# Batch 1's context gate from token pairs, with the weight sums and the steps of x taken by GpSimd in the opening

## The chip, the core and the metric

The kernel runs on one core of one Trainium2 chip. Its engines are TensorE (PE, matrix products), ScalarE (ACT), VectorE (DVE), GpSimd (POOL) and SyncE (SP, which here only issues DMAs). The metric is device time in microseconds (us). The kernel before took 1031.0 us, the median of three runs (1030.94 to 1032.0).

## The reference

Eight batches of 512 tokens with 256 channels pass two layers, each added to its input. What matters for the change is the first layer's context gate:

```python
ctx = causal_ema(x, tau_ctx)              # h[t] = alpha * h[t-1] + x[t]
wg = sigmoid(concat([x, ctx]) @ Wg.T + bg)
gated = x * wg
# then: mod = 0.5 + sigmoid(W2 gelu(W1 x)); eight EMAs of gated * mod, blended, a second gate,
# a projection and a layer norm; x2 = x + that
```

The second layer runs five feed-forward networks per batch (three shared, two experts chosen by the batch's type), each 256 to 1024 to 256 with a relu, and mixes them by a small gate.

## The kernel before, in words

Channels lie on partitions, in two tiles of 128 (CT = 2); tokens lie along the free dimension. Products are exact to nearly fp32: every operand is split into a high part and a low part (`hi` on ACT, `lo` on DVE), and `product` adds three products (high x high, high x low, low x high).

**The mixture sets the pace.** A batch of the second layer is 40 slots. In slot k PE runs `up(k + 2)` (six products into one of four banks `ps_up`), then `down(k)` (six products). Between them ACT computes the relu as the high part `hid_hi` and DVE the low part `hid_lo`; there are four buffers of each. In batch 0 the weights too are split on the way (`wi_round`, `wo_round` on ACT, `wi_rest`, `wo_rest` on DVE) and stored for the later batches.

**The first layer of the next batch runs beside it.** While batch b of the mixture runs, the first layer of batch n = b + 1 is cut into named steps. A plan for each engine says in front of which slot a step stands (k), or behind it (k + 0.5). `FIRST_PLANS` (L82 to L106) is the plan of n = 1, which runs beside batch 0; `PLAN_...` are those of the later ones. Each engine takes its instructions in this order, whatever is ready. A step's `ema_in` and `ema_out` on DVE are the eight EMAs, from slot 3.5 to 23.5 in batch 0.

**The context gate.** Since the EMA is linear, the gate's product can be taken before the scan. For n = 1 (`wgate`, L862) PE takes x and x one token back: for each of two output tiles, four terms of three products of 512 columns (`gate_product`, L810). DVE scans the result out of PSUM (`gate_scan`). For n > 1 the tokens are held apart as evens and odds (256 columns each), and there are two steps: `gate_mid` (L842) multiplies the even tokens by the sum of the two weight matrices, 12 products of 256 columns; `wgate` (L852) multiplies the steps of x (differences of neighbouring tokens) by each weight matrix, 24 products of 256 columns. ACT copies the first result out, DVE adds it to the second and scans (L1524).

**Their inputs.** The summed weights (`mid_raw`) come from `add_gate_weights` on GpSimd (L1929): three additions of 128x512, late in batch 0, between its DMAs for the experts' weights; ACT and DVE split them in slot 38. The steps come from `next_steps` on DVE (L1507): for each channel tile one instruction of one element and two of 255 and 256. ACT and DVE split these too (`next_steps_hi`, `next_steps_lo`).

**The opening.** Before batch 0's mixture can start, the first layer of batch 0 runs alone (to about 54 us). DVE's sixteen scans (L1780) set its pace; the inputs of EMAs 1 to 4 come from PSUM, those of EMAs 0 and 5 to 7 from SBUF (5 to 7 multiplied by GpSimd, L1945). The last one is scanned in halves, with `open_total_end` (L1789) between. Then come a gate, a projection, a layer norm and the split of x2 (`x2_round` on ACT). In the opening x of batch 1 is split as well (`x1_hi`, `x1_lo`), and its soma and hidden layer are computed.

**Between batches**, DVE's `add_expert_b` (L1401) adds the last expert out of `ps_down`; PE's first `down` of the next batch waits for it.

## Time and profile before

| what | value |
|---|---|
| median of three runs | 1031.0 us |
| the profiled execution's own time | 1030.5 us |
| its span (first to last instruction) | 1028.6 us |
| PE busy | 1019.8 us (99%), 4840 products |
| DVE busy | 838.7 us (82%), 1495 instructions |
| ACT busy | 425.7 us (41%) |
| POOL busy | 21.1 us (2%), 29 instructions |
| clock granted to PE | 0.998 of full speed |

The page gives busy time for each engine; a busy PE is not a PE at its peak, since the ends of its products are modelled. Where an engine waited, the list of waits says for whom. The timeline gives single instructions in order of time.

### The profile page before, as it was taken

What the parts mean: (1) busy time and instruction counts of PE and PEld (TensorE: products, weight loads), DVE (VectorE), ACT (ScalarE), POOL (GpSimd) and SP (SyncE); (2) the same over time, 40 slices, a digit from 0 to 9 for tenths busy, and PEclk for the clock granted to TensorE, in tenths of its full rate; (3) what the DMA queues carried; (4) which work ended last, traced back from release to release, by engine and by line L of the source; (5) the groups of instructions that cost most, each with busy time, mean ns of one, the idle gap of its engine ahead of it and who ended that gap; (6) DMA issues with size and microseconds to landing.
All of it is one profiled execution on the core that took longest, in us unless ns stands there. A gap on an engine that the chain in (4) does not pass through costs nothing.

```text
span 1028.6 us, 13022 instructions
## 1 busy us (share of the span) xinstructions
PE 1019.8 (99%) x4840; PEld 850.4 (83%) x4840; DVE 838.7 (82%) x1495; ACT 425.7 (41%) x707; POOL 21.1 (2%) x29
## 2 busy tenths in 40 slices
PE   8999999999999999999999999999999999999998
PEld 6688887888888888888888888888888888888898
DVE  6989978799788988789886997869977799755237
ACT  8654456533444233542435234442334423332232
POOL 1200011000000000000000000000000000000000
PEclk9999999999999999999999999999999999999999
DMA  6387899687354664456544674546645466455682
GB/s 216 104 302 289 304 367 354 251 322 264 135 197 169 242 242 162 165 200 229 192 182 148 236 254 156 205 164 225 231 158 204 165 242 220 141 196 190 220 323 86
DMA packets 38305, 222.53 MB, mean 216 GB/s; under 512 B 4642, under 2 KB 5410, under 8 KB 16610
## 3 DMA queue, kind: packets, MB, share of 16 engines
q1 hardware_dynamic: 35938, 209.12, 56.9%
q0 software_dynamic: 2304, 12.58, 3.1%
q8 instruction: 38, 0.62, 0.2%
q14 instruction: 25, 0.20, 0.1%
HBM read 188.00 MB, written 33.69 MB: 216 GB/s over the span
## 4 chain that ended last, share of the span: by engine, by line
PE 95%; DVE 3%; DMA 1%; issue 0%; ACT 0%; SPq 0%; DVEq 0%; ACTq 0%
PE ps_down L776 14%; PE ps_up L704 14%; PE ps_down L780 14%; PE ps_up L735 14%; PE ps_down L777 14%; PE ps_up L734 14%; PE ps_aux L697 2%; PE ps_aux L698 2%; PE ps_aux L699 2%; DVE y L1780 1%; PE ps_aux L896 1%; PE ps_aux L893 1%; PE ps_aux L892 1%; PE ps_aux L876 1%; PE ps_aux L877 1%; PE ps_aux L881 1%
## 5 line engine op out<-in xcount | busy, mean ns | idle before, releaser
L1111 ACT ACTIVATE hid_hi<-ps_up 128x512 fp32r<-128x512 f32 (+1 forms) x336 | 193.5, 577 | 473.5 <-PE ps_up L704 472.6
L1386 DVE SCALAR_TENSOR_TENSOR hid_lo<-ps_up,hid_hi 128x512 fp32r<-128x512 f32 (+1 forms) x336 | 218.6, 656 | 134.7 <-ACT hid_hi L1111 133.2
L734 PE MATMUL ps_up<-x_hi_all,wi 128*128 128x512 f32 (+1 forms) x660 | 250.0, 381 | 0.0
L735 PE MATMUL ps_up<-x_hi_all,wi 128*128 128x512 f32 (+1 forms) x660 | 249.9, 380 | 0.0
L776 PE MATMUL ps_down<-hid_hi,wo 128*128 128x512 f32 (+1 forms) x640 | 245.9, 385 | 2.3 <-DVE y L1406 2.2
L777 PE MATMUL ps_down<-hid_hi,wo 128*128 128x512 f32 (+1 forms) x640 | 245.5, 385 | 0.0
L704 PE MATMUL ps_up<-x_lo_all,wi 128*128 128x512 f32 (+1 forms) x660 | 197.3, 380 | 0.2 <-DVE x_lo_all L1377 0.2
L780 PE MATMUL ps_down<-hid_lo,wo 128*128 128x512 f32 (+1 forms) x640 | 194.2, 385 | 0.0
L734 PEld LDWEIGHTS ps_up<-x_hi_all,wi 128*128 128x128 f32 x660 | 124.1, 188 | 23.4 <-issue 0.2
L735 PEld LDWEIGHTS ps_up<-x_hi_all,wi 128*128 128x128 f32 x660 | 124.1, 188 | 23.0
L776 PEld LDWEIGHTS ps_down<-hid_hi,wo 128*128 128x128 f32 x640 | 120.5, 188 | 27.4 <-issue 2.9
L704 PEld LDWEIGHTS ps_up<-x_lo_all,wi 128*128 128x128 f32 x660 | 122.0, 188 | 24.3 <-DVE x_lo_all L1377 0.4
L777 PEld LDWEIGHTS ps_down<-hid_hi,wo 128*128 128x128 f32 x640 | 120.6, 188 | 23.4
L780 PEld LDWEIGHTS ps_down<-hid_lo,wo 128*128 128x128 f32 x640 | 119.3, 188 | 24.1 <-DVE hid_lo L1386 0.2
L1496 DVE TENSOR_TENSOR_SCAN trace<-alpha,trace 128x512 f32<-128x512 f32 x98 | 118.8, 1213 | 0.0
L1565 DVE SCALAR_TENSOR_TENSOR trace<-modb,blend_w,gates 128x512 f32<-128x512 f32 x98 | 68.7, 741 | 0.0
L1574 DVE TENSOR_TENSOR temporal<-trace,temporal 128x512 f32<-128x512 f32 x98 | 62.0, 672 | 0.0
L1612 DVE STREAM_TRANSPOSE temporal<-normed 32x256 f32<-32x256 f32 x96 | 41.9, 436 | 4.1 <-DVEq L1605 1.3
L1453 DVE SCALAR_TENSOR_TENSOR x<-y,g,x 128x512 f32<-128x512 f32 x56 | 38.8, 744 | 0.0
L1124 ACT ACTIVATE y<-ps_down 128x512 f32<-128x512 f32 x48 | 26.1, 596 | 18.5 <-PE ps_down L780 18.5
L1238 ACT ACT_TABLE_LOAD x25 | 32.1, 1283 | 0.4
L1424 DVE SCALAR_TENSOR_TENSOR gpart<-gw,y,gpart 128x256 f32<-128x256 f32 x40 | 19.4, 485 | 1.4
(283 smaller groups left out, 967.4 us busy)
## 6 DMA issues: line engine op xcount, KB each, us to landing
wi<-split_wi SPq DMA_DIRECT2D x70, 1024.0 KB, 4.8
wo<-split_wo SPq DMA_DIRECT2D x70, 1024.0 KB, 4.8
modb<-mod_scratch SPq DMA_DIRECT2D x28, 512.0 KB, 5.8
split_wi<-wi SPq DMA_DIRECT2D x10, 1024.0 KB, 7.4
split_wo<-wo SPq DMA_DIRECT2D x10, 1024.0 KB, 7.9
xt<-in_x SPq DMA_DIRECT2D x8, 512.0 KB, 6.1
split_wi<-ex POOLq DMA_DIRECT2D x4, 1024.0 KB, 9.2
split_wo<-ex POOLq DMA_DIRECT2D x4, 1024.0 KB, 6.3
```

The costliest lines, as they stand in the source:

```text
L704: mm = pe.matmul(ps, w_hi[c], x2_lo[:, parity, c, tokens], start=False, stop=c == CT - 1)
L734: pe.matmul(ps, w_hi, x2_hi[:, parity, c, tokens], start=c == 0, stop=False)
L735: pe.matmul(ps, w_lo, x2_hi[:, parity, c, tokens], start=False, stop=False)
L776: pe.matmul(bank, w_hi[:, cols], hid_hi[:, at % NU, tokens], start=start, stop=False)
L777: pe.matmul(bank, w_lo[:, cols], hid_hi[:, at % NU, tokens], start=False, stop=False)
L780: mm = pe.matmul(bank, w, hid_lo[:, at % NU, tokens], start=False, stop=stop)
L1111: act.activation(hid_hi[:, k % NU, tokens], ps_up[k % NU][:, tokens], ACT.Relu).then_inc(hid_hi_ready, 1)
L1386: dve.scalar_tensor_tensor(hid_lo[:, k % NU, tokens], ps_up[k % NU][:, tokens], 0.0, f32(hid_hi[:, k % NU, tokens]), ALU.max, ALU.subtract ...
L1496: scan = dve.tensor_tensor_scan(trace_of(d)[:, c, :], alpha[:, d:d + 1].broadcast_to([P, T]), trace_of(d)[:, c, :], 0.0, ALU.mult, ALU.add)
L1565: dve.scalar_tensor_tensor(trace_of(d)[:, c, :], modb[:, d // 2 % 2, d % 2, :], blend_w[:, c, d:d + 1], gates[:, c, :], ALU.mult, ALU.mult ...
L1574: dve.tensor_tensor(temporal[:, c, :], trace[:, c, :], temporal[:, c, :], ALU.add).then_inc(ema_sum, 1)
L1612: dve.transpose(turned[quarter(b), a], unturned[quarter(a), b]).then_inc(quarter_moved, 1)
```

## The change

Batch 1's gate is computed as that of the later batches: `gate_mid` behind slot 1 and `wgate` ahead of slot 2 on PE; ACT copies the middle out in slot 2, DVE adds and scans behind slot 2 instead of ahead of it. For that x of batch 1, its soma and its mod are laid out as evens and odds. GpSimd sums the weights in the opening, into `temporal`, behind its first two DMA issues and once the second trace is summed, and right after it takes the steps of batch 1's x. ACT splits both between the two x2 rounds of the opening, DVE behind the first two `hid_lo`. GpSimd also takes the steps of batch 2's x, once the EMAs of batch 1 are done; DVE has them no more in slot 38.5 of batch 0. From batch 2 on nothing changes. The diff, with most unchanged lines left out:

```diff
...
     "sync": from_slot(PLAN_SYNC, 8, {1: ["mod"], 1.5: ["modb0", "modb1"]}),
-    "tensor": {0.5: ["mod"], 1.5: ["wgate"], 27.5: ["tgate"], 30: ["out"], 33.5: ["turn"]},
-    "scalar": {0.5: ["mod"], 2: ["wgate"], 26: ["temp_hi"], 28: ["tgate"], 29: ["sg_hi"],
-               31: ["ln_sqrt"], 34.5: ["turn"], 35.5: ["x2_hi"], 37: ["next_x_hi", "table_gelu"], 38: ["mid_weights"], 39: ["next_steps_hi"]},
-    "vector": {2: ["wgate_scan", "gated"],
+    "tensor": {0.5: ["mod"], 1.5: ["gate_mid"], 2: ["wgate"], 27.5: ["tgate"], 30: ["out"], 33.5: ["turn"]},
+    "scalar": {0.5: ["mod"], 2: ["gate_mid"], 2.5: ["wgate"], 26: ["temp_hi"], 28: ["tgate"], 29: ["sg_hi"],
+               31: ["ln_sqrt"], 34.5: ["turn"], 35.5: ["x2_hi"], 37: ["next_x_hi", "table_gelu"], 38: ["next_steps_hi"]},
+    "vector": {2.5: ["wgate_scan", "gated"],
                26: ["temp_lo"], 28.5: ["sg"], 29: ["sg_lo"], 30.5: ["ln_stats"], 31.5: ["ln_norm"], 35: ["x2"], 36: ["x2_lo"],
-               37.5: ["next_x_lo"], 38.5: ["mid_weights", "next_steps"], 39.5: ["next_steps_lo"]},
+               37.5: ["next_x_lo"], 38.5: ["next_steps_lo"]},
...
         gate_mid = trace[:, 0, :]
-        mid_raw, mid_raw_part = (raw_wi[:, 0, i * CT * E:(i + 1) * CT * E] for i in range(2))
+        mid_raw, mid_raw_part = temporal[:, 0, :], temporal[:, 1, :]
...
             return xt[n % 2][:, :, :]
+
+        def take_steps(eng, n):
+
+            for c in range(CT):
+                even, odd = (evens_odds(x_of(n)[:, c, :])[:, s, :] for s in range(2))
+                to_even, to_odd = (token_steps[:, c, half(s)] for s in range(2))
+                eng.tensor_scalar(to_even[:, 0:1], even[:, 0:1], -1.0, None, ALU.mult)
+                eng.tensor_tensor(to_even[:, 1:HALF], odd[:, 0:HALF - 1], even[:, 1:HALF], ALU.subtract)
+                last = eng.tensor_tensor(to_odd, odd, even, ALU.subtract)
+            last.then_inc(steps_ready, 1)
...
                 elif step == "gate_mid":
-                    if n == 2:
+                    if n == 1:
                         pe.wait_ge(mid_weights, 5)
+                    xh, xl = (xg_hi, xg_lo) if n > 1 else (x1_hi, x1_lo)
                             at = slice(c * E + m * P, c * E + (m + 1) * P)
-                            mm = product(ps_aux[1][:, half(m)], mid_hi[:, at], mid_lo[:, at], xg_hi[:, c, half(0)],
-                                         xg_lo[:, c, half(0)], m == 0 and c == 0, m == CT - 1 and c == CT - 1)
+                            mm = product(ps_aux[1][:, half(m)], mid_hi[:, at], mid_lo[:, at], xh[:, c, half(0)],
+                                         xl[:, c, half(0)], m == 0 and c == 0, m == CT - 1 and c == CT - 1)
                     mm.then_inc(aux_ready[1], 1)
-                elif step == "wgate" and n > 1:
-                    pe.wait_ge(steps_ready, (n - 1) * 3)
+                elif step == "wgate":
+                    pe.wait_ge(steps_ready, n * 3)
                     for m in range(CT):
-                        pe.wait_ge(aux_free[m], p.aux[m]["wgate"])
+                        if later(p.aux[m]["wgate"]):
+                            pe.wait_ge(aux_free[m], p.aux[m]["wgate"])
                         mm.then_inc(aux_ready[m], 1)
-                elif step == "wgate":
-                    for m in range(CT):
-                        if later(p.aux[m]["wgate"]):
-                            pe.wait_ge(aux_free[m], p.aux[m]["wgate"])
-                        gate_product(ps_aux[m], m, x1_hi_all, x1_lo_all, EDGE1).then_inc(aux_ready[m], 1)
...
                 elif step == "next_steps_hi":
-                    act.wait_ge(steps_ready, (n - 1) * 3 + 1)
+                    act.wait_ge(steps_ready, n * 3 + 1)
                     hi(steps_hi, token_steps).then_inc(steps_ready, 1)
-                elif step == "mid_weights":
-                    act.wait_ge(mid_weights, 3)
-                    hi(mid_hi, mid_raw).then_inc(mid_weights, 1)
                 elif step == "gate_mid":
-                    act.wait_ge(steps_ready, (n - 1) * 3)
+                    act.wait_ge(steps_ready, n * 3)
...
                     if n == 1:
-                        act.activation(mod[:, :], ps_aux[1][0:D, :], ACT.Sigmoid, bias=par[0:D, C_BN2:C_BN2 + 1])\
+                        act.activation(evens_odds(mod), apart(ps_aux[1][0:D, :]), ACT.Sigmoid, bias=par[0:D, C_BN2:C_BN2 + 1])\
...
                     for c in range(CT):
-                        if n == 1:
-                            act.wait_ge(aux_free[c], p.aux[c]["wgate"] + 1)
-                        else:
-                            act.wait_ge(gate_scanned, (n - 2) * CT + c + 1)
+                        act.wait_ge(gate_scanned, (n - 1) * CT + c + 1)
...
                     act.wait_ge(x_loaded[1], 16)
-                    hi(both(x1_hi), both(x_of(1))).then_inc(open_x1_hi, 1)
+                    for c in range(CT):
+                        last = hi(apart(x1_hi[:, c, :]), evens_odds(x_of(1)[:, c, :]))
+                    last.then_inc(open_x1_hi, 1)
...
                 x2_round(0)
+                act.wait_ge(mid_weights, 3)
+                hi(mid_hi, mid_raw).then_inc(mid_weights, 1)
+                act.wait_ge(steps_ready, 1)
+                hi(steps_hi, token_steps).then_inc(steps_ready, 1)
...
                     act.wait_ge(open_x1_done, (1, 3)[c])
-                    act.activation(soma[:, c, :], ps_aux[c][:, :], ACT.Gelu, bias=col(C_BSOMA, c)).then_inc(open_soma1, 1)
+                    act.activation(evens_odds(soma[:, c, :]), apart(ps_aux[c][:, :]), ACT.Gelu, bias=col(C_BSOMA, c)).then_inc(open_soma1, 1)
...
                     dve.wait_ge(ema_sum, n * (2 * D))
-                    for c in range(CT):
-                        even, odd = (evens_odds(x_of(n + 1)[:, c, :])[:, s, :] for s in range(2))
-                        to_even, to_odd = (token_steps[:, c, half(s)] for s in range(2))
-                        dve.tensor_scalar(to_even[:, 0:1], even[:, 0:1], -1.0, None, ALU.mult)
-                        dve.tensor_tensor(to_even[:, 1:HALF], odd[:, 0:HALF - 1], even[:, 1:HALF], ALU.subtract)
-                        last = dve.tensor_tensor(to_odd, odd, even, ALU.subtract)
-                    last.then_inc(steps_ready, 1)
+                    take_steps(dve, n + 1)
                 elif step == "next_steps_lo":
-                    dve.wait_ge(steps_ready, (n - 1) * 3 + 2)
+                    dve.wait_ge(steps_ready, n * 3 + 2)
                     lo(steps_lo, token_steps, steps_hi).then_inc(steps_ready, 1)
-                elif step == "mid_weights":
-                    dve.wait_ge(mid_weights, 4)
-                    lo(mid_lo, mid_raw, mid_hi).then_inc(mid_weights, 1)
-                elif step == "wgate_scan" and n > 1:
+                elif step == "wgate_scan":
...
                                                ALU.mult, ALU.add).then_inc(gate_scanned, 1)
-                elif step == "wgate_scan":
-                    for c in range(CT):
-                        dve.wait_ge(aux_ready[c], p.aux[c]["wgate"] + 1)
-                        gate_scan(c).then_inc(aux_free[c], 1)
-                        if c == 0:
+                        if n == 1 and c == 0:
...
                 dve.wait_ge(open_x1_hi, 1)
-                lo(x1_lo, x_of(1), x1_hi).then_inc(open_x1_split, 1)
+                for c in range(CT):
+                    last = lo(apart(x1_lo[:, c, :]), evens_odds(x_of(1)[:, c, :]), apart(x1_hi[:, c, :]))
+                last.then_inc(open_x1_split, 1)
...
             relu_lo(0, 1)
+            dve.wait_ge(mid_weights, 4)
+            lo(mid_lo, mid_raw, mid_hi).then_inc(mid_weights, 1)
+            dve.wait_ge(steps_ready, 2)
+            lo(steps_lo, token_steps, steps_hi).then_inc(steps_ready, 1)
...
-                pool.wait_ge(wi_ready, UNITS - 1)
+                pool.wait_ge(open_sum, 2 * CT)
...
             load_tile(1)
+            add_gate_weights()
+            pool.wait_ge(x_loaded[1], 16)
+            take_steps(pool, 1)
...
                 if j == 0:
-                    add_gate_weights()
+                    pool.wait_ge(x_loaded[0], 32)
+                    pool.wait_ge(ema_sum, 2 * D)
+                    take_steps(pool, 2)
...
```

## Rows read from the trace of the kernel before

**Rows 1.** The page, busy time and share of the span of each engine
```profile
PE 1019.8 (99%) x4840; PEld 850.4 (83%) x4840; DVE 838.7 (82%) x1495; ACT 425.7 (41%) x707; POOL 21.1 (2%) x29
```

**Rows 2.** Waits of PE, whole span: us in total, times, longest
```profile
PE ps_down L776 <- DVE y L1406: 2.2, 1, 2.2
```

**Rows 3.** Timeline of PE (start, us): gate of batch 1, of batch 2
```profile
59.98 0.40 PE L697 MATMUL ps_aux<-x_hi_all,wc_hi 128*128 128x512 f32 x1
65.52 0.39 PE L734 MATMUL ps_up<-x_hi_all,wi 128*128 128x512 f32 x1
...
198.45 0.28 PE L697 MATMUL ps_aux<-ct_hi,wc_hi 128*128 128x256 f32 x1
201.32 0.40 PE L734 MATMUL ps_up<-x_hi_all,wi 128*128 128x512 f32 x1
```

**Rows 4.** Timeline of ACT: second x2 round, then the splits in slot 38
```profile
51.41 0.81 ACT L1073 ACTIVATE x_hi_all<-x 128x256 fp32r<-128x256 f32 x2 [1.15 <-DVE x L1824]
...
169.89 0.62 ACT L1073 ACTIVATE mid_parts<-raw_wi 128x512 fp32r<-128x512 f32 x1
175.12 1.06 ACT L1073 ACTIVATE ct_hi<-trace 128x1024 fp32r<-128x1024 f32 x1 [2.82 <-DVE trace L1516]
```

**Rows 5.** Timeline, PE and DVE in slots 2 to 4; batch 2's addition
```profile
68.27 0.39 PE L734 MATMUL ps_up<-x_hi_all,wi 128*128 128x512 f32 x1
...
65.72 1.22 DVE L1487 TENSOR_TENSOR_SCAN gates<-alpha,ps_aux 128x512 f32<-128x512 f32 x1 [0.42 <-PE ps_aux L699]
67.73 0.69 DVE L1553 TENSOR_TENSOR gates<-gates,xt 128x512 f32<-128x512 f32 x1 [0.21 <-ACT gates L1195]
70.46 0.69 DVE L1386 SCALAR_TENSOR_TENSOR hid_lo<-ps_up,hid_hi 128x512 fp32r<-128x512 f32 x1 [1.43 <-ACT hid_hi L1111]
71.06 1.22 DVE L1377 TENSOR_TENSOR wi<-raw_wi,wi 128x1024 fp32r<-128x1024 f32 x1
72.19 1.41 DVE L1565 SCALAR_TENSOR_TENSOR temporal<-modb,blend_w,gates 128x512 f32<-128x512 f32 x2
...
200.50 0.69 DVE L1528 TENSOR_TENSOR gates<-ps_aux,trace 128x512 f32<-128x512 f32 x1 [0.57 <-PE ps_aux L699]
```

**Rows 6.** Stretches: us, busy by engine (instructions), granted clock, DMA share, GB/s
```profile
90.00:100.90 10.90, 10.90 (x49) 9.01 (x48) 10.90 (x16) 4.32 (x7) 0.00 (x0) 1.00 0.84 298
180.00:183.00 3.00, 3.00 (x10) 2.33 (x9) 1.39 (x4) 0.00 (x0) 0.00 (x0) 0.58 0.41 169
```

**Rows 7.** Timeline of DVE and of PE, slot 26 of batch 0
```profile
132.38 1.27 DVE L1386 SCALAR_TENSOR_TENSOR hid_lo<-ps_up,hid_hi 128x512 fp32r<-128x512 f32 x2
...
133.18 0.68 PE L780 MATMUL ps_down<-hid_lo,wo 128*128 128x512 f32 x2
```

**Rows 8.** Timeline of DVE and of PE, from batch 0 to batch 1
```profile
178.44 1.40 DVE L1406 SCALAR_TENSOR_TENSOR y<-ps_down,wa_now,y 128x512 f32<-128x512 f32 x2
...
179.33 0.77 PE L776 MATMUL ps_down<-hid_hi,wo 128*128 128x512 f32 x1 [2.22 <-DVE y L1406]
```

**Rows 9.** Timeline of POOL and of DVE, near 153 us
```profile
152.83 1.30 POOL L1934 TENSOR_TENSOR raw_wi<-wc_hi 128x512 f32<-128x512 f32 x1
154.21 2.18 POOL L1936 TENSOR_TENSOR raw_wi<-raw_wi 128x512 f32<-128x512 f32 x1
...
153.58 1.64 DVE L1377 TENSOR_TENSOR wi<-raw_wi,wi 128x1024 fp32r<-128x1024 f32 x1
```

**Rows 10.** Timeline of POOL and of DVE in the opening
```profile
22.78 7.42 POOL L1945 TENSOR_TENSOR y<-hid_lo,gates 128x512 f32<-128x512 f32 x6 [22.09 <-DMA hid_lo<-open_mod_scratch]
30.14 1.26 POOL L1918 DMA_DIRECT2D ex<-in_expert_wi  x2
...
27.36 4.53 DVE L1780 TENSOR_TENSOR_SCAN y<-alpha,ps_up 128x512 f32<-128x512 f32 x4
31.80 5.71 DVE L1780 TENSOR_TENSOR_SCAN y<-alpha,y 128x512 f32<-128x512 f32 x6
37.43 0.85 DVE L1789 SCALAR_TENSOR_TENSOR y<-y,blend_w,ps_down 128x256 f32<-128x256 f32 x2
```

## The prediction

> **What bounds the kernel now.** I read the busy shares first: TensorE (PE) is busy 99% of the span [rows 1], so time is saved only where PE works less or waits less. The list of what PE waited for has one entry of weight, 2.2 us in one piece, for `add_expert_b` on VectorE (DVE) [rows 2]. The other views say where PE's queue is nearly late without showing as a wait. In the opening (to 54 us) DVE runs the sixteen decaying scans and what follows them back to back. In batch 0 DVE has no idle time from 70 us to past 133 us; the stretch 90 to 100.9 shows it busy 10.90 of 10.90 [rows 6]. There PE is only just not late: the two `hid_lo` that started at 132.38 took 1.27 for the pair, so the first was done at about 133.0, and PE began to use it at 133.18, with that pair of products stretched to 0.68 [rows 7]. So the slack of PE against DVE is about nothing in slot 26 of batch 0. Any DVE work added before that slot is paid in full; what is taken off PE before it is given back as a wait.
>
> **1. The products of batch 1's gate.** Before: 24 products of 512 columns, from 59.98 to 65.52, 5.54 us. After: 12 + 24 products of 256 columns. 24 such take 2.87 us in the next batch (198.45 to 201.32) [rows 3], so 36 take 4.30. PE's work falls by 1.24 us.
>
> **2. Two more splits on ScalarE (ACT) in the opening.** The high parts of the summed weights (0.62) and of the steps (1.06) [rows 4] go between the first x2 round and the table load, ahead of the second x2 round. That round had waited 1.15 us for DVE [rows 4]. 1.68 - 1.15 = 0.53 is the dearest; consecutive ACT instructions overlap by about 0.1 each, which makes it about 0.34. With the opening's x split now in two instructions I take **+0.4**. The strided outputs (soma, mod) follow behind it and have cover in PE's first two slots. PE starts `gate_mid` at 59.98 + 0.4 = 60.4 and the sigmoid of mod, which frees its bank, comes before that. The copy of the middle (about 0.6 us on ACT) has the first bank's 12 products as cover (1.4 us).
>
> **3. DVE in slots 0 to 4 of batch 0.** Added: the low parts of the weights (about 0.6) and of the steps (1.1), and an addition of 0.69 ahead of each of the two gate scans [rows 5]. Moved: the scans go behind the `hid_lo` of slot 2, so DVE first stands idle until PE, ACT and that `hid_lo` have had their turn. That idle time hides the two low parts. PE reaches slot 2 at 65.52 + 0.4 - 1.24 = 64.68. In slot 3 `hid_lo` starts 70.46 - 68.27 = 2.19 us after PE's first product [rows 5], so here it starts at 66.87. Behind it, up to the first input of the EMA: `hid_lo` 0.60, addition 0.69, scan 1.13, the late weights' low part 1.13, addition 0.69, from the second scan's start to the second gating 67.73 - 65.72 = 2.01, gating 0.60, `hid_lo` 0.60, `wi_rest` 1.13 (differences of starts in [rows 5]; the scan's 1.13 is a quarter of the 4.53 in [rows 10], the late part has `wi_rest`'s shape). That is 8.58, so the EMA starts at 75.45, not at 72.19 [rows 5]: DVE is **3.3 us** later. It has no idle time to absorb this until slot 26, and there PE has no slack. So PE too is 3.3 late after slot 26; this contains the +0.4 and swallows the -1.24. Bounds: 2.5 if a few tenths of slack are hidden in it, 3.9 if the order costs one `hid_lo` more. The waits would come in pieces under 1 us from slot 6 on, as the slack runs out.
>
> **4. The end of batch 0.** Before, the chain is: steps of x on DVE, their high part on ACT after a wait of 2.82 us for them [rows 4], ACT's relu behind that, `hid_lo`, the steps' low part, and only then `add_expert_b` at 178.44; PE stood 2.22 us before 179.33 [rows 8]. The clock granted to PE then falls to 0.58 between 180 and 183 [rows 6]: 3 us at 0.42 less is 1.26, and the first product at 179.33 took 0.77 us where others take 0.39 [rows 8, 3], which with its neighbour makes some 0.3 more. The change takes the weights and the steps off DVE here, and ACT's high part finds the steps long done. Nothing else is late: `add_expert_b`'s first half then has PE's 1.4 us of `up` as cover. **-2.2 - 1.6 = -3.8.** If the clock falls elsewhere instead, in the new waits of point 3, 1.6 comes back.
>
> **5. GpSimd beside the scans.** This is the doubtful part, and it decides the sign. GpSimd's three additions of 128x512 and the six instructions of `take_steps` start when its two DMA issues end, at 30.14 + 1.26 = 31.40, just before DVE's scans that read SBUF alone (31.80) [rows 10]. Beside the scans that read PSUM, six GpSimd multiplications ran at 1.27 each and the scans kept their 1.13: nobody paid [rows 10]. But once in this trace GpSimd met a DVE instruction that reads both inputs from SBUF. GpSimd's second addition ran until 152.83 + 1.30 = 154.13; the DVE subtraction issued at 153.58 took 1.64 instead of 1.21 and ended at 155.22; GpSimd's third addition, issued at 154.21, took 2.18 and ended at 156.39 [rows 9]. These are the times of three instructions run strictly one after the other: 154.13 + 1.1, then 155.22 + 1.2. The scans from 31.80 on read alpha and their input from SBUF, so I expect the same of them: whoever is waiting goes next, scan and GpSimd in turn, and the opening hangs on the scans. GpSimd's time: 3 x 1.30 = 3.9; four half-size subtractions at about half of that plus a start, 0.69 each, 2.8 (estimate; 0.65 to 1.30 by the shapes in [rows 9, 10]); two one-element instructions, at most 0.2 each, 0.3. Together 7.0. Off it: the 0.40 before the first scan wants to start, and about 0.8 beside the two blending instructions that read PSUM (0.85) [rows 10]. **+5.8**, one to one, since DVE is continuous from there to the end of the opening.
>
> The Trainium skill (SBUF — State Buffer, section Who interferes with whom) states this as a rule: a VectorE instruction with two SBUF inputs and a GpSimd instruction that reads SBUF exclude each other for a whole instruction, and the one that issues second waits. The additions in [rows 9] agree for a subtraction; no row shows it for a scan. By the rule the scans pay, and the same 5.8 comes out.
>
> **Sum.** 3.3 - 3.8 + 5.8 = +5.3. The profiled execution took 1030.5 us (a span of 1028.6 and 1.9 around it), 0.5 below the median of 1031.0. So 1035.8 by its own time, **1036.3** against the median. GpSimd's steps for batch 2 (about 3 us near 152) fall where DVE has idle time, and cost nothing; without that cover at most 0.7.
>
> **The rivals.** (a) *The scans don't pay, or pay less.* A scan might not need what the subtraction needed: 1031.0 - 0.5 = 1030.5. Or DVE's queued instruction wins over a waiting GpSimd each time, and only first meetings cost: 31.80 to 32.70 for the first scan, and about 0.5 each where GpSimd gets in beside a blending and holds up a half scan or the gating: 1.9, giving 1032.4. For it: no row shows two DVE instructions in a row with GpSimd waiting. Both are within 0.2% of before. (b) *Faster: DVE's delay in batch 0 finds slack that I don't see.* Then -1.24 + 0.4 - 3.8 and no loss at the scans: 1026.4. Decided by whether `hid_lo` is late by slot 26; against it, [rows 6, 7]. (c) *Slower still:* strided half-size subtractions cost GpSimd as much as full ones, +2.4, and PE's clock falls in the longer gaps between the trace sums as it did after the 2.2 us wait, +1.5: 1040.2. (d) *The change doesn't do what it says:* the 36 products run no faster than 24 because loading weights limits them; [rows 3] exclude it.
>
> **How the numbers follow.** Forecast (all three terms as above) 0.53; (a) 0.27; (b) 0.07; (c) 0.13. The range goes from below (a) to (c): 1030.0 to 1040.0, and leaves out (b) and part of (c). A measurement of this kernel can tell about 0.2% (2.1 us) from no change. Slower by more: 0.53 + 0.13, less a little at the edge, 0.65. Same: (a) and that edge, 0.27. Faster 0.08.
>
> **What would show it.** Point 1: products of 256 columns between slot 1 and slot 2, 4.3 us in all. Point 2: the second x2 round 0.3 to 0.5 later than DVE's residual. Point 3: `ema_in0` some 8.1 us behind the first product of slot 3 instead of 3.9, and PE waiting for `hid_lo` or `wi` from slot 6 to 26 by 4.1 us in all, none of it before slot 6. Point 4: no wait for `add_expert_b`, full clock there. Point 5: scans with SBUF input that take 1.9 to 2.5 us instead of 1.2 while GpSimd works, GpSimd additions of over 2 us, and the opening longer by 5 to 6 us. The prediction is wrong in the main if those scans keep 1.2 us (then 1030.5), or if PE shows no wait for `hid_lo` (then point 3 falls).

## The result and the profile after

| | before | after |
|---|---|---|
| median (runs) | 1030.05 us (20) | 1033.53 us (20) |
| lowest to highest | 1028.57 to 1032.28 | 1032.07 to 1034.79 |
| span of the profiled execution | 1028.6 us | 1032.2 us |
| ratio, 95% interval | | 1.0032 [1.0025, 1.0039] |

The change makes the kernel 3.5 us slower. The page after, busy time of each engine, to be held against [rows 1]:

```profile
PE 1021.6 (99%) x4852; PEld 849.2 (82%) x4852; DVE 844.0 (82%) x1493; ACT 427.1 (41%) x710; POOL 31.2 (3%) x41
```

GpSimd has twelve instructions and 10 us more. DVE has two instructions fewer and yet 5.3 us more busy time. Where it comes from stands in the timeline of POOL and of DVE in the opening (start, duration), beside [rows 10]:

```profile
26.88 4.53 DVE L1774 TENSOR_TENSOR_SCAN y<-alpha,ps_up 128x512 f32<-128x512 f32 x4
31.33 9.60 DVE L1774 TENSOR_TENSOR_SCAN y<-alpha,y 128x512 f32<-128x512 f32 x6
44.54 0.76 DVE L1789 TENSOR_TENSOR gates<-gates,soma 128x256 f32<-128x256 f32 x2
...
31.73 2.29 POOL L1934 TENSOR_TENSOR temporal<-wc_lo 128x512 f32<-128x512 f32 x1
34.00 2.17 POOL L1934 TENSOR_TENSOR temporal<-wc_hi 128x512 f32<-128x512 f32 x1
36.25 2.06 POOL L1936 TENSOR_TENSOR temporal<-temporal 128x512 f32<-128x512 f32 x1
38.29 1.12 POOL L455 TENSOR_SCALAR trace<-xt 128x1 f32<-128x1 f32 x1
39.38 1.00 POOL L456 TENSOR_TENSOR trace<-xt 128x255 f32<-128x255 f32 x1
40.34 0.99 POOL L457 TENSOR_TENSOR trace<-xt 128x256 f32<-128x256 f32 x1
...
41.48 0.61 POOL L456 TENSOR_TENSOR trace<-xt 128x255 f32<-128x255 f32 x1
42.04 0.61 POOL L457 TENSOR_TENSOR trace<-xt 128x256 f32<-128x256 f32 x1
```

The four scans out of PSUM keep their 4.53. The six scans from SBUF (four of 512 columns and two of 256, which this view counts as one group) take 9.60 instead of 5.71, while GpSimd's additions take over 2 us instead of 1.3, and even its instruction on one element takes 1.12: both engines stand in turn. From the first scan out of PSUM to the gating with soma it is 44.54 - 26.88 = 17.66 us. Before it was 12.92, from the scan in [rows 10] to this line:

```profile
40.28 0.75 DVE L1795 TENSOR_TENSOR gates<-gates,soma 128x256 f32<-128x256 f32 x2
```

The opening is **4.74** longer.

The waits of PE (what it waited for, us in total, times, longest), beside [rows 2]:

```profile
PE ps_down L946 <- DVE y L1774: 2.8, 3, 1.0
PE ps_down L790 <- DVE hid_lo L1393: 1.4, 4, 0.6
...
PE ps_up L744 <- DVE wi L1384: 0.8, 2, 0.4
```

The 2.2 us wait for `add_expert_b` is gone. Three waits for scans in the opening and six short ones in the mixture have come.

Slots 1 to 3 of batch 0, timelines of PE, of ACT and of DVE, beside [rows 3, 5]:

```profile
64.43 0.28 PE L707 MATMUL ps_aux<-x_hi_all,mid_parts 128*128 128x256 f32 x1
...
68.73 0.40 PE L744 MATMUL ps_up<-x_hi_all,wi 128*128 128x512 f32 x1
...
71.48 0.39 PE L744 MATMUL ps_up<-x_hi_all,wi 128*128 128x512 f32 x1
...
70.32 0.60 ACT L1118 ACTIVATE hid_hi<-ps_up 128x512 fp32r<-128x512 f32 x1 [3.60 <-PE ps_up L714]
...
70.95 0.69 DVE L1393 SCALAR_TENSOR_TENSOR hid_lo<-ps_up,hid_hi 128x512 fp32r<-128x512 f32 x1 [2.26 <-ACT hid_hi L1118]
71.56 0.68 DVE L1526 TENSOR_TENSOR gates<-ps_aux,trace 128x512 f32<-128x512 f32 x1
72.27 1.23 DVE L1530 TENSOR_TENSOR_SCAN gates<-alpha,gates 128x512 f32<-128x512 f32 x1
...
79.61 1.41 DVE L1559 SCALAR_TENSOR_TENSOR temporal<-modb,blend_w,gates 128x512 f32<-128x512 f32 x2
```

And the end of batch 0, one stretch (us, busy by engine, granted clock, DMA share, GB/s) beside [rows 6], and the first product of `mod_hidden`, after and before:

```profile
180.00:183.00 3.00, 3.00 (x15) 2.48 (x14) 2.10 (x3) 0.60 (x1) 0.55 (x1) 1.00 1.00 419
...
185.76 0.39 PE L840 MATMUL ps_aux<-xg_hi_all,wc_hi 128*128 128x512 f32 x1
```

```profile
182.03 0.62 PE L830 MATMUL ps_aux<-xg_hi_all,wc_hi 128*128 128x512 f32 x1
```

**The account.** The first product of `mod_hidden`, with which batch 1 gets going, started at 182.03 before and at 185.76 after, 3.73 later; the whole span is 3.6 longer. (Of the time, 1.9 us lie outside the span before and 1.6 after; why is open.) Cut at four marks: up to the first scan out of PSUM -0.48 (27.36 to 26.88; nothing of the change lies there); from there to the gating +4.74; to the first `hid_lo` of batch 0 (55.12 before, 59.56 after) +0.18 (14.84 to 15.02); to the first input of the EMAs +2.98 (17.07 to 20.05); to `mod_hidden` -3.69 (109.84 to 106.15). So everything happens before batch 1, and three terms make it: the opening, DVE's delay in slots 2 to 4, and the wait that went.

PE's own starts say where it pays DVE's delay. The first product of `down` in each slot lies 3.21 us later than before in slots 2 to 5, 4.23 in slot 7, 5.57 in slot 10, 7.38 in slot 18 and 7.43 from slot 27 to 39. That last figure is DVE's delay at the EMAs' input (79.61 - 72.19 = 7.42). So between slots 5 and 27 PE gives up 4.22 us. The list of waits has only 2.2 of it, because it counts from the modelled end of the product before. An example is slot 9, where the last two products of `down` and the next `up` start 1.13 us apart, which is 0.67 more than twice the usual 0.23; the list says 0.40:

```profile
91.60 0.73 PE L790 MATMUL ps_down<-hid_lo,wo 128*128 128x512 f32 x2
92.73 0.50 PE L744 MATMUL ps_up<-x_hi_all,wi 128*128 128x512 f32 x1 [0.40 <-DVE wi L1384]
```

### The profile page after: what moved, and what is told of

It is laid out like the page before. It is cut to its first block, busy times and chain, and to the rows that moved or that the text cites. A ratio compares the mean times of both kernels' runs of the same rounds, so it can differ in the third digit from the quotient of the medians.

```text
span 1032.2 us, 13061 instructions
## 1 busy us (share of the span) xinstructions
PE 1021.6 (99%) x4852; PEld 849.2 (82%) x4852; DVE 844.0 (82%) x1493; ACT 427.1 (41%) x710; POOL 31.2 (3%) x41
## 4 chain that ended last, share of the span: by engine, by line
PE 90%; DVE 8%; ACT 1%; DMA 1%; issue 1%; SPq 0%; DVEq 0%
PE ps_up L714 13%; PE ps_down L786 13%; PE ps_down L790 13%; PE ps_up L744 13%; PE ps_up L745 13%; PE ps_down L787 13%; PE ps_aux L707 2%; PE ps_aux L708 2%; PE ps_aux L709 2%; DVE y L1774 1%; DVE hid_lo L1393 1%; DVE trace L1503 1%; PE ps_aux L903 1%; PE ps_aux L900 1%; PE ps_aux L899 1%; PE ps_aux L884 1%
```

## The experiments

The kernel before ran beside each of them, at 1030.1 to 1030.4 us.

### What GpSimd costs in the opening

**e1_writes_only.** The changed kernel, with GpSimd's nine instructions in the opening replaced by memsets of the same shapes. Batch 1's gate is thus computed from zeros.

```diff
-                for t, place in ((wc_lo, mid_raw), (wc_hi, mid_raw_part)):
-                    pool.tensor_tensor(place, ...).then_inc(mid_weights, 1)
+                for place in (mid_raw, mid_raw_part):
+                    pool.memset(place, 0.0).then_inc(mid_weights, 1)
...
-            take_steps(pool, 1)
+            for c in range(CT):
+                pool.memset(token_steps[:, c, 0:1], 0.0)
...
```

> The changed kernel, but GpSimd's nine instructions in the opening are fills of the same shapes: they write SBUF and read nothing (batch 1's gate is then computed from zeros, so its numbers are left out). Theory 'turns': scans with both inputs in SBUF and GpSimd instructions that read SBUF take turns, and only that cost the 4.7 us by which the opening grew. Then the six scans from the fifth EMA on keep 5.7 us in all and the time is 1033.5 - 4.7 = 1028.8. Rival 'presence': whatever GpSimd does beside the scans costs, or the growth came from the waits on its semaphores: 1033.5, scans still near 2.1 us each.

Measured: 1030.2 us (1028.8 to 1031.6), ratio to before 0.9991 [0.9980, 1.0003]. The timeline of POOL and DVE:

```profile
30.89 1.00 POOL L1934 MEMSET temporal<- 128x512 f32 x2
31.95 0.52 POOL L1936 MEMSET temporal<- 128x512 f32 x1
...
31.79 5.71 DVE L1774 TENSOR_TENSOR_SCAN y<-alpha,y 128x512 f32<-128x512 f32 x6
```

Seven of the nine memsets lay beside these scans (the first two at 30.89 did not), and the scans have their 5.71 back. From the first scan out of PSUM to the gating it is 40.26 - 27.34 = 12.92, as before. Memsets are shorter than additions, but those beside the scans took 1.6 us (31.95 to 33.55), and none of it came on top. So what costs is that GpSimd reads. The time is 1.4 above the expectation; the interval is wide enough for most of that.

**e2_after_scans.** The changed kernel, with the same work of GpSimd held back until DVE has split the first weights of the mixture; steps first, then weights, and ACT's split of the weights behind the table load.

```diff
             load_tile(1)
-            add_gate_weights()
+            pool.wait_ge(wi_ready, 1)
+            pool.wait_ge(open_sum, 2 * CT)
             pool.wait_ge(x_loaded[1], 16)
             take_steps(pool, 1)
+            add_gate_weights()
```

> The changed kernel with GpSimd's work in the opening held back until DVE has done the low part of the first wi, steps first, weights second; ACT splits the steps before and the weights behind its table load. DVE's work from there on reads mostly PSUM. Turns: the scans run free, what is left is a piece of at most 0.7 us beside the split of x2: 1029.0 (1028.7 to 1029.7). Presence: the same 7 us of GpSimd beside DVE cost the same wherever they lie: 1033.5.

Measured: 1029.2 us (1028.6 to 1030.7), ratio 0.9984 [0.9974, 0.9994]. GpSimd now works from 43.82 to 50.7 us, and six scans take 5.71. So 4.3 of the changed kernel's time is the place of GpSimd's work (the order of its two jobs and one split on ACT moved along with it), and nothing else in the change needed that place. (From the gating to the first `hid_lo` it is 15.22, 0.2 more than in the changed kernel.)

### How the two engines share

**e5_three_adds and e6_six_adds.** The kernel before, with three or six additions of 128x512 on GpSimd, whose result nothing uses, right behind its two DMA issues.

```diff
             load_tile(1)
+            for i in range(3):
+                if i > 1:
+                    pool.wait_ge(mid_weights, i - 1)
+                pool.tensor_tensor(ex[:, 0, 0, ...], f32(wc_lo[:, ...]), f32(wc_lo[:, ...]), ALU.add).then_inc(mid_weights, 1)
```

> The kernel before, with three additions of 128x512 more on GpSimd behind its first two DMA issues, beside the scans; their results are used by nothing. In the changed kernel the starts of the scans moved from 1.13 to 2.15 us apart, 1.02 per addition, though an addition lasts 1.3. Turns: 3 x 1.02 = +3.1, so 1033.1. Rival 'full length': each costs its own 1.3: +3.9, 1033.9. Presence by share: both slow down a little while together, under +1.

> The same with six additions. Turns: the fourth meets the last full scan, the later ones the half scans and the blending, which reads PSUM and lets one addition of the two last ones by: 5 x 1.02 = +5.1, 1035.1, between +4.1 and +6.1. Full length: +6.5 to +7.8. If PE's clock falls in the longer gaps, up to 1.5 more.

Measured: 1034.9 us (1.0052 [1.0035, 1.0070]) and 1038.9 us (1.0084 [1.0066, 1.0101]), 4.5 and 8.5 above before. Both are more than the 1.02 per addition that I had taken from the changed kernel. The timeline of the run of three shows a behaviour that the changed kernel did not:

```profile
30.86 3.72 POOL L1957 TENSOR_TENSOR ex<-wc_lo 128x512 f32<-128x512 f32 x3
...
31.02 9.17 DVE L1782 TENSOR_TENSOR_SCAN y<-alpha,y 128x512 f32<-128x512 f32 x6
```

GpSimd went through its three additions at 1.24 each, and the scan, issued 0.16 after the first of them, did not get in between; in the run of six it went through six (7.38). There were no turns. That left the question of what decides between turns and going through. In the changed kernel the scan had been first (31.33, then 31.73). In this run GpSimd was first. Three more kernels, all with three additions:

**e9_adds_with_gaps.** Each addition waits for the end of the one before, so that there is a gap between them (`if i: pool.wait_ge(mid_weights, i)`).

> The run of three unused additions again, GpSimd first as there, but each addition waits for the end of the one before it, so that GpSimd has a short gap between any two. Theory (a gap lets the waiting scan in): the first addition 1.25, the others about 2.1 each, six scans about 8.9. Rival (who began first keeps the turn): all three 1.25 plus the gap, scans 9.2 or more as in the run without gaps.

**e8_adds_later.** No gaps, but two memsets of 0.5 ahead of the additions.

> The kernel before with three unused GpSimd additions of 128x512 in the opening, as in the run of three, but with two GpSimd memsets (0.5 each) ahead of them, so that the first addition comes after the first scan with SBUF input has begun. Theory (who comes first decides: if a scan has the turn, scan and addition alternate and each addition costs the six scans 1.0): additions of 2.0 to 2.3 each, six scans 8.8 us, opening +3.0, 1033.5 us. Rival (GpSimd without gaps keeps DVE out once it is in): the first addition about 2, the next two 1.25 each, six scans 9.2 to 9.5, 1034.5 or more.

**e11_adds_second.** No gaps, and four memsets ahead.

> As the run with two memsets ahead of the three unused additions, but with four (0.5 each), since with two of them the first addition was still issued (32.58) just before the first scan with SBUF input could begin (about 33.0) and GpSimd went through its three additions in one go, 1.24 each. Here the scan is first, and there is no gap between the additions. Theory (who is first decides; if it is the scan, they take turns): additions of 2.0 to 2.3 each, not 1.24, six scans about 8.8 to 9.1. Rival (GpSimd without gaps keeps DVE out once it has got in): the first addition about 2, the next two 1.24.

Measured: e9 1033.5 us (1.0036 [1.0021, 1.0050]), e8 1034.2 us (1.0042 [1.0027, 1.0058]), e11 1034.5 us (1.0042 [1.0031, 1.0053]). In e8 the two memsets were not enough: its first addition was issued at 32.58, 0.38 before the group of scans, so that GpSimd was first again, and the run doesn't test what it was meant for. GpSimd again went through, at 1.27 each. In the two others, the additions' line (duration in ns, smallest, median, largest; first and last start), e9 first, e11 below:

```profile
L1957 POOL TENSOR_TENSOR ex<-wc_lo x3: 1290/2062/2073, 31.3 to 34.8; 128x512 f32<-128x512 f32 x3
```

```profile
L1960 POOL TENSOR_TENSOR ex<-wc_lo x3: 1677/2175/2179, 31.4 to 35.1; 128x512 f32<-128x512 f32 x3
```

In e11 the scans began at 30.77, ahead of the first addition at 31.35, and though there is no gap between the additions every one of them had to wait for a scan. That is the theory's half "who is first decides", and its rival (the second and third at 1.24) falls. In e9, with gaps, the second and third addition waited, and the first did not (1.29). By the starts alone the scan would have been first there (31.12, GpSimd at 31.26), but the scan's duration says otherwise:

```profile
31.12 2.52 DVE L1782 TENSOR_TENSOR_SCAN y<-alpha,y 128x512 f32<-128x512 f32 x1
```

Its record begins while the scan before it still runs (to 31.21), and it ends at 33.64, 1.09 behind the end of the first addition (31.26 + 1.29 = 32.55). So GpSimd was first as in e5, and what differs from e5 is the gap: here each gap let a scan in. That is the other half. e3 agrees with it: there GpSimd is first with two additions without a gap at 1.28 and 1.27, and then comes the third, which waits for their end, at 2.07. Each is a single trace, and starts that lie within some 0.15 us of each other don't tell who was first. The three additions of e3:

```profile
31.77 1.28 POOL L1934 TENSOR_TENSOR temporal<-wc_lo 128x512 f32<-128x512 f32 x1
33.01 1.27 POOL L1934 TENSOR_TENSOR temporal<-wc_hi 128x512 f32<-128x512 f32 x1
34.36 2.07 POOL L1936 TENSOR_TENSOR temporal<-temporal 128x512 f32<-128x512 f32 x1
```

What it costs hardly depends on this. Against 5.71, the six scans grew by 3.46 and 3.24 where GpSimd went through (e5, e8), by 3.37 and 3.08 where they took turns (e9, e11), and by 7.19 for six: **1.0 to 1.2 us for each addition that takes 1.25 alone.**

In the changed kernel the starts of the scans split the growth: 1.03 for each of the three additions, 0.37 for each of two half-size subtractions (the second lengthens a half scan of the last EMA, behind the six), nothing for the rest, and 0.43 by which the very first of these scans took longer (1.63, from 31.33, instead of 1.20) though no addition ran before it. What held that one is open.

The Trainium skill (SBUF — State Buffer, section Who interferes with whom) has a VectorE instruction with two SBUF inputs contend with a GpSimd instruction that reads SBUF, and not with one that only writes it. The runs now agree for scans too: 9.60 with reads, 5.71 with memsets. That GpSimd goes on over several instructions of its own while a scan waits is more than the page states.

### A second cost: TensorE's clock

The opening of e6 grew by 8.46 though its scans grew by 7.19. The rest is in PE's rows. Stretches of 4 us (PE, PEld, DVE, ACT, POOL busy, then the granted clock), after e5, then e11:

```profile
32.00:36.00 4.00, 1.59 (x5) 0.55 (x4) 4.00 (x2) 2.07 (x3) 2.59 (x3) 0.97 0.54 212
36.00:40.00 4.00, 4.00 (x6) 1.64 (x7) 4.00 (x5) 0.00 (x0) 0.00 (x0) 0.60 0.00 0
```

```profile
32.00:36.00 4.00, 3.12 (x7) 0.87 (x5) 4.00 (x2) 1.84 (x2) 4.00 (x3) 1.00 0.20 81
36.00:40.00 4.00, 2.19 (x4) 0.59 (x4) 4.00 (x6) 0.00 (x0) 1.31 (x1) 1.00 0.00 0
```

In e5 PE waited 2.4 us for a scan in one piece, and the granted clock of the next stretch is 0.60 of full speed, that is, for most of it the lower of its two levels (1.2 of 2.4 GHz). In e6, where PE waited 6.1 in one piece, a whole stretch is at 0.50. In the traced execution of e11 the same three additions in turns gave three waits, 1.0 at most, and no fall. A table of all openings; "growth" is against 5.71 and against 12.92 from the first scan out of PSUM to the gating, the clock is the lowest of the stretches of 4 us from 32 to 44, all in the one traced execution of each kernel:

| kernel | six scans grew | opening grew | difference | clock |
|---|---|---|---|---|
| e11, turns | 3.08 | 3.08 | 0.00 | 1.00 |
| e9, turns | 3.37 | 3.37 | 0.00 | 1.00 |
| e3 (as the changed kernel) | 3.91 | 4.00 | 0.09 | 1.00 |
| e8, GpSimd goes through | 3.24 | 3.97 | 0.73 | 0.67 |
| e5, GpSimd goes through | 3.46 | 4.26 | 0.80 | 0.60 |
| changed kernel | 3.89 | 4.74 | 0.85 | 0.66 |
| e6, six | 7.19 | 8.46 | 1.27 | 0.50 |

Where the clock fell, DVE's blending instructions had to wait for PE's late products (0.39 before one of them in the changed kernel), and 0.7 to 1.3 came on top. Of the changed kernel's 0.85, 0.37 is not the clock's: a half-size subtraction lengthened a half scan, 1.76 for the pair instead of 1.39. e3's 0.09 is of that kind too.

The table shows what a fall costs, and not that turns avoid it. The traced execution of e11 was the fastest of its eight (1031.2 us, where the median is 1034.5), and its mean clock was 1.000. Four of the eight had 0.997, which in e5's trace stands for two falls (one at the end of batch 0); none of the 77 executions of the kernel before is that low. And e11's median is no lower than those of e5 and e8.

### What work on DVE costs in batch 0

**e10_two_more_dve.** The kernel before, with two subtractions of 128x1024 on DVE that nothing uses, ahead of the first input of the EMAs.

```diff
                     if d == 0:
                         dve.wait_ge(gated_ready, n * 2 + 2)
+                        if n == 1:
+                            for place in (temporal, trace):
+                                dve.tensor_tensor(both(place), both(x_of(1)), both(x_of(1)), ALU.subtract).then_inc(spare, 1)
```

> The kernel before with two unused DVE subtractions of 128x1024 (1.13 apart, 2.26 in all) ahead of the first input of batch 1's EMAs, behind the hid_lo of slot 3; nothing else moves. Theory (DVE and PE have no slack in batch 0 up to slot 26, so that work added on DVE is paid in full): 1030.4 + 2.3 = 1032.7, with some 2.3 us of new waits of PE for hid_lo or wi between slots 6 and 26. Rival (there is slack, and what the changed kernel lost there came from elsewhere): 1030.4 to 1031.0.

Measured: 1032.2 us (1030.2 to 1034.5), ratio 1.0026 [1.0016, 1.0035]: 2.05 for 2.26 us of work. DVE in slot 26, beside [rows 7], and PE's new waits:

```profile
133.51 1.30 DVE L1387 SCALAR_TENSOR_TENSOR hid_lo<-ps_up,hid_hi 128x512 fp32r<-128x512 f32 x2
```

```profile
PE ps_down L781 <- DVE hid_lo L1387: 0.9, 2, 0.7
PE ps_up L735 <- DVE wi L1378: 0.4, 1, 0.4
```

Counted from the first `hid_lo` of batch 0 (54.00 here, 55.12 before), this pair is at 79.51 instead of 77.26: 2.25 later after 60 us. Nothing was absorbed on the way. PE is as late: from that first `hid_lo` to the first product of `mod_hidden` it takes 128.11 us (54.00 to 182.11), against 126.91 before (55.12 to 182.03), though the last products ahead of it ran in 1.60 here (180.51 to 182.11) and in 2.70 before (179.33 to 182.03), where the clock had fallen. 1.20 + 1.10 = 2.30. The new waits that the list names make only 1.3 of that, but by the starts of the first `down` product of each slot PE gives up 2.23 us in three pieces (0.41 to slot 10, 0.97 to slot 17, 0.85 to slot 18), and 0.06 more to slot 27. The rival, slack, falls.

**e3_scan_slot2.** The changed kernel, with ACT's `wgate` and DVE's `wgate_scan` and `gated` in slot 2, ahead of its `hid_lo`.

```diff
-    "scalar": {0.5: ["mod"], 2: ["gate_mid"], 2.5: ["wgate"], ...
+    "scalar": {0.5: ["mod"], 2: ["gate_mid", "wgate"], ...
-    "vector": {2.5: ["wgate_scan", "gated"],
+    "vector": {2: ["wgate_scan", "gated"],
```

> The changed kernel with one edit in the plan: batch 1's gate scans and their sigmoid stand ahead of slot 2 again, as before the change, and not behind it. Theory 'queue': of DVE's 3.0 us of delay at the first EMA input 2.3 are its idle time in front of the hid_lo of slot 2, and PE pays DVE's delay in full by slot 26; so 1033.5 - 2.3 = 1031.2, with PE's waits for hid_lo and wi down from 2.2 us to near zero. Rival: the added instructions are the cost and the idle time is absorbed later: 1033.5.

Measured: 1032.3 us (1030.8 to 1033.3), ratio 1.0010 [1.0001, 1.0020]: 1.2 below the changed kernel, half of what I expected. DVE's timeline says where the other half is:

```profile
68.57 0.68 DVE L1526 TENSOR_TENSOR gates<-ps_aux,trace 128x512 f32<-128x512 f32 x1
...
76.20 0.69 DVE L1393 SCALAR_TENSOR_TENSOR hid_lo<-ps_up,hid_hi 128x512 fp32r<-128x512 f32 x1 [0.63 <-ACT hid_hi L1118]
...
77.94 1.41 DVE L1559 SCALAR_TENSOR_TENSOR temporal<-modb,blend_w,gates 128x512 f32<-128x512 f32 x2
```

The idle time of 2.26 before the `hid_lo` is gone, but DVE is now so early that it stands 0.63 for ACT before the next `hid_lo`. From the first `hid_lo` (59.53) to the EMAs' input it is 18.41 us, against 20.05 in the changed kernel and 17.07 before: 1.64 came back, not 2.26. The mechanism held, and the expectation counted the idle time that goes but not the one that comes.

### The parts that pay

**e4_steps2_alone.** The kernel before, with one part of the change alone: GpSimd takes batch 2's steps behind its weight sums, and DVE no more in slot 38.5.

```diff
-               37.5: ["next_x_lo"], 38.5: ["mid_weights", "next_steps"], 39.5: ["next_steps_lo"]},
+               37.5: ["next_x_lo"], 38.5: ["mid_weights"], 39.5: ["next_steps_lo"]},
...
                 if j == 0:
                     add_gate_weights()
+                    pool.wait_ge(x_loaded[0], 32)
+                    pool.wait_ge(ema_sum, 2 * D)
+                    take_steps(pool, 2)
```

> The kernel before, with only this part of the change: GpSimd takes the steps of batch 2's x behind its sums of the weights, near 155 us, and DVE has them no more in slot 38.5 of batch 0. By the prediction's point 4 the wait for add_expert_b (2.2 us) and the slow clock behind it (1.6 us) both go: 1030.0 - 3.8 = 1026.2. Rival: the clock falls anyway in that place, or only the wait goes: 1027.8. Second rival: the weights' split in slot 38 keeps ACT and DVE late, and little changes: 1029.5.

**e7_both.** The changed kernel with the edits of e2 and e3 together.

> The changed kernel with both remedies: GpSimd's work behind the scans, and the gate scans ahead of slot 2. If the two costs are separate they add: 1033.5 - 4.7 - 2.3 = 1026.5, which beats both kernels. If PE's slack against DVE in batch 0 had been eaten by the opening's delay and not by DVE's own, the second remedy gives nothing once the first is in: 1028.8.

Measured: e4 1026.7 us (1026.2 to 1028.5), ratio 0.9960 [0.9945, 0.9976]; e7 1027.7 us (1027.4 to 1030.8), ratio 0.9980 [0.9970, 0.9990]. Both beat both kernels, and **e4 is the best of all, 3.7 below before and 6.9 below the change.** In its end of batch 0, the first product that waited for `add_expert_b`, and the stretch around it:

```profile
176.62 0.47 PE L786 MATMUL ps_down<-hid_hi,wo 128*128 128x512 f32 x1 [0.58 <-DVE y L1416]
...
175.00:178.00 3.00, 2.42 (x11) 1.52 (x10) 3.00 (x6) 1.66 (x2) 0.00 (x0) 1.00 0.96 345
```

The wait is 0.58 instead of 2.22 [rows 8], and the clock stays at 1.00. From the EMAs' input to `mod_hidden` it is 107.08 us, 2.75 less than before; the whole change has 3.69 less there. So the steps alone bring three quarters of the gain at this place. Rewriting batch 1's gate, which is what forces work into the opening and into slots 2 to 4, adds 0.9 to that gain and costs more ahead of it. Even with GpSimd well placed and the scans early (e7), from the gating to the EMAs' input it is 33.63 us, against 31.94 in e4, and by the medians e7 is 1.0 slower. The intervals of the two ratios touch, so the traces carry this more than the medians do (152.72 against 151.93 us from the first scan out of PSUM to `mod_hidden`).

## Why the prediction was right, and where its sizes were off

The sign, the forecast case and the three terms held. The change costs 3.5 us (1030.05 to 1033.53) where the sum said 5.3. The forecast of 1036.3 is 2.8 too high: 1.0 because its base, the median of three runs, was 1031.0, where 20 runs give 1030.05, and 1.8 in the difference. Of these, 1.1 is in the terms (5.3 for 3.16 - 3.69 + 4.74 = 4.21), nearly all of it in point 5; 0.48 is the start of the opening, which varies from trace to trace, and 0.3 lies outside the span.

**Point 1 (products), -1.24: as predicted.** 64.43 to 68.73 is 4.30, as the sum said. It was swallowed as said, since PE waits for DVE afterwards.

**Point 2 (ACT), +0.4: smaller.** Gating to the first `hid_lo` grew by 0.18. The second x2 round on ACT came 0.75 behind DVE's result (55.16 to 55.91), the difference from before being 0.24, below my bound of 0.34.

**Point 3 (DVE in slots 2 to 4), 3.3 with point 2's 0.4 in it: measured 0.18 + 2.98 = 3.16.** The marker I named, `ema_in0` 8.1 us behind the first product of slot 3, came out at 8.13 (71.48 to 79.61). That DVE has no slack up to slot 26 is shown by e10. The 4.1 us that I expected PE to give up from slot 6 on are there: by its starts it is 4.22, none of it before slot 6, though the list of waits has only 2.2. So the term and its mechanism were right.

**Point 4 (end of batch 0), -3.8: measured -3.69 in the traces, with the parts a little different.** The last `down` of batch 0 starts 2.38 earlier against the products before it (the list's wait was 2.22). From there to `mod_hidden` it takes 1.38 (184.38 to 185.76) instead of 2.70. e10, with the same wait and no fall of the clock, takes 1.60, so 1.10 of the 1.32 is the clock's and 0.22 is a slower start behind a wait. Behind `mod_hidden` the slow clock cost 0.27 more, up to the next `down`. It cost 1.37 in all where I had 1.6. e4, which moves batch 2's steps alone, gained 3.7 by the medians (2.5 to 5.7 by its interval) and 2.75 in this stretch of its trace. And the clock's share holds only for the usual execution. In 54 of 77 executions of the kernel before that ran beside these experiments the mean granted clock was 0.998, in 23 it was 1.000, and the medians of the two kinds lie 1.2 to 2.0 us apart in each of the four sets. e10 kept the wait of 2.23, and its trace shows no fall after it:

```profile
180.51 0.47 PE L777 MATMUL ps_down<-hid_hi,wo 128*128 128x512 f32 x1 [2.23 <-DVE y L1407]
```

This product took 0.47, where the same one after the same wait took 0.77 in [rows 8], and the stretch from 180 to 183 stands at 1.00. In e1, e2, e4 and e7, in which this wait is gone (in e4, down to 0.58) and which have none of GpSimd's reads beside the scans, 39 of 40 executions had 1.000 and one 0.999. The changed kernel had 1.000 in 13 of 20 (median 1032.7) and 0.998 or 0.999 in seven (0.998: 1034.6), in the traced one from the opening. So the change took the clock's fall away from the end of batch 0, and in a third of the executions one came back, as the trace shows it where PE waits for the scans. The prediction had that only as part of rival (c).

**Point 5 (GpSimd beside the scans), +5.8: the mis-sized term, 4.74 in the trace.** The mechanism, turns at the SBUF reads, was right, and rival (a) with it wrong: no case of the scans getting by for nothing. The size was wrong because I took GpSimd's work one to one, 7.0 less 1.2. It was 6.6 alone (half-size subtractions take 0.61, not 0.69). The additions cost the scans 1.03 each, 3.1 in all, where the sum had 3.9 less 0.4. The six small instructions cost 0.37 twice, 0.74, where the sum had 3.1 less 0.8: two of the subtractions lengthened a scan and the others did not, and the last three instructions (0.20, 0.61, 0.61) ran mostly beside the blending out of PSUM. With the 0.43 of the first scan, which is unexplained, the scans paid 3.89 + 0.37 = 4.3. The other 0.5 is PE's, mainly the 0.39 for which a blending waited, with PE at 0.66 of its clock, which the sum did not have at all. "Whoever is waiting goes next" was also too simple: three traces show GpSimd taking three or six turns running.

**Rival (b)** (slack absorbs DVE's delay, 1026.4) falls with e10. **(c)** was right in one of its two causes, the clock, and not in the other, since half-size subtractions took half. **(d)** fell as said.

## What to carry to other kernels

Work on an engine that stands idle is free only where it reads nothing that the pacing engine wants at that moment: GpSimd's readings of SBUF beside two-input instructions of DVE cost nearly their full length, and the same work 12 us later cost 0.2 at most. When a change bundles a move and a rewrite, price each alone against the chain that ends last; here one move of six small instructions had three quarters of the gain, and the rewrite, which took 1.24 us off an engine that then had to wait, had the costs. Look for idle time that an early step creates elsewhere before counting on what it frees.

## What the runs showed of the hardware that I had not expected

- GpSimd can keep DVE's two-input instructions out over several of its own: 3.72 us for three additions and 7.38 for six, with a scan waiting all the while. A gap between its additions let a scan in (e9: 1.29, 2.07 and 2.06, where e5 without gaps has 3.72 for all three). If the scan was first, they alternate even without gaps on GpSimd's side (e11: 1.68, 2.18 and 2.18 for the three).
- Memsets of GpSimd beside those scans cost them nothing (5.71 for six).
- The scan out of PSUM has only its factor in SBUF and keeps 1.13 beside GpSimd's multiplications; the scan from SBUF takes 2.2 beside its additions.
- One wait of PE of 2.2 us brings its clock down in some executions (0.58 over the 3 us in [rows 6]) and not in others (e10); three waits of about 1.0 at most in the opening did so in one trace (the changed kernel, 0.66) and not in three others (e3, e9, e11). What decides between them stays open.
